# A graph layer pair on one core: one-hot tables made six tiles at a time, basis parts spread anew

## What is computed

```python
# layer 0
xw = x @ W.T
out = segment_sum(dinv[row] * dinv[col] * xw[row], col) + b
x = _layernorm(x + gelu(batch_norm(out)) + x)

# layers 1 and 2: rgcn_gate_layer
w = einsum('rb,bio->rio', att, basis)      # 30 matrices of 512 x 512, 2 relations
for r in range(2):
    gate = sigmoid(x_j @ gate_w[r, :, 0])
    msgs.append(gate[:, None] * x_j @ w[r])
msg = where(edge_type == 0, msgs[0], msgs[1])
out = segment_sum(msg, row) + x @ root + bias
```

## Time and profile before

| | us |
|---|---|
| median of 3 runs (327.39, 329.15, 327.48) | 327.48 |
| the profiled execution, whole | 326.88 |
| its span, first to last instruction | 325.0 |
| PE busy / DVE busy / ACT busy | 283.5 / 175.3 / 135.3 |
| mean granted TensorE clock | 0.942 of full |
| moved by DMA | 73.68 MB |

### The profile page before, as it was taken

How to read it: one execution, slowest core, us unless ns; L and a number is a source line. 1 busy time by engine, 2 the same in 40 slices (tenths; PEclk the granted TensorE clock), 3 DMA queues, 4 the chain that set the end, 5 groups by cost and what they waited for, 6 DMA issues and landing times.

```text
span 325.0 us, 4963 instructions
## 1 busy us (share of the span) xinstructions
PE 283.5 (87%) x1711; PEld 193.4 (60%) x1711; DVE 175.3 (54%) x538; ACT 135.3 (42%) x265; POOL 36.5 (11%) x71
## 2 busy tenths in 40 slices
PE   1768899885969999568999999999997999999991
PEld 1653455432336786424767656647795777787771
DVE  3878787999967847686310132233325125433333
ACT  4596868899701368647243114111313142100000
POOL 1001000000002900551000000000003600010000
PEclk9987999998695999779999999999998999999997
DMA  6974869599997999739998677975001400001112
GB/s 175 335 327 158 336 257 356 207 388 416 352 385 282 314 354 418 313 103 367 382 381 318 260 292 303 418 294 246 2 0 32 132 0 0 2 0 33 33 34 63
DMA packets 12759, 73.68 MB, mean 227 GB/s; under 512 B 1952, under 2 KB 2195, under 8 KB 4540
## 3 DMA queue, kind: packets, MB, share of 16 engines
q1 hardware_dynamic: 11282, 70.82, 57.4%
q0 software_dynamic: 1104, 2.36, 2.8%
q10 hardware_dynamic: 346, 0.17, 0.3%
HBM read 72.05 MB, written 1.28 MB: 226 GB/s over the span
## 4 chain that ended last, share of the span: by engine, by line
PE 61%; DVE 22%; issue 7%; DMA 4%; DVEq 2%; ACT 1%; POOL 1%; ACTq 0%; POOLq 0%
PE psW L495 13%; PE psM L476 10%; PE psM L477 9%; PE psM L478 9%; PE psM L717 6%; PE psM L737 6%; DVE oh_key L1047 4%; DMA basis_ring<-in_L_gnn_basis_dram 3%; PE psM L623 3%; DVE B L1038 2%; PE psE L570 2%; DVEq L1032 2%; DVE w L1027 1%; DVE x_sum L1170 1%; DVE AT L1103 1%
## 5 line engine op out<-in xcount | busy, mean ns | idle before, releaser
L495 PE MATMUL psW<-basis_ring,S 128*32 128x512 f32 x512 | 68.2, 651 | 3.2 <-DMA basis_ring<-in_L_gnn_basis_dram 3.1
L1217 DVE SCALAR_TENSOR_TENSOR zg<-psM,gate,zg 125x512 fp32r<-125x512 f32 x20 | 15.0, 751 | 59.5 <-ACT zg L891 59.5
L1047 DVE TENSOR_SCALAR oh_key<-iota_f,key 128x160 f16<-128x160 f16 x162 | 36.0, 262 | 2.6 <-PE psE L570 1.4
L785 ACT ACTIVATE oh_diff<-iota_f,edgeT 128x128 f16<-128x128 f16 x108 | 34.1, 389 | 3.4 <-DVEq L964 3.4
L495 PEld LDWEIGHTS psW<-basis_ring,S 128*32 128x32 f32 x512 | 13.9, 115 | 32.5 <-issue 26.4
L476 PE MATMUL psM<-w,hlT 128*125 128x512 f32 x80 | 33.1, 414 | 0.1
L891 ACT ACTIVATE zg<-psM,gate 125x512 fp32r<-125x512 f32 x20 | 13.8, 688 | 46.1 <-PE psM L478 45.7
L477 PE MATMUL psM<-w,hlT 128*125 128x512 f32 x80 | 32.3, 404 | 0.0
L478 PE MATMUL psM<-w,hlT 128*125 128x512 f32 x80 | 32.1, 402 | 0.0
L570 PEld LDWEIGHTS psE<-oh_key,oh_src 128*125 128x125 f16 x162 | 16.0, 150 | 25.2 <-issue 19.2
L570 PE MATMUL psE<-oh_key,oh_src 128*125 128x160 f16 x162 | 21.3, 261 | 10.2 <-issue 6.6
(11 more groups left out here) (159 smaller groups left out, 430.5 us busy)
## 6 DMA issues: line engine op xcount, KB each, us to landing
basis_ring<-in_L_gnn_basis_dram SPq DMA_DIRECT2D x64, 1024.0 KB, 7.1
root_raw<-in_L_gnn_root_dram POOLq DMA_DIRECT2D x32, 64.0 KB, 3.6
xs<-in_x_dram SPq DMA_DIRECT2D x1, 1120.0 KB
out_dram<-xs SPq DMA_DIRECT2D x5, 224.0 KB
w_raw<-in_L_gnn_W_dram SPq DMA_DIRECT2D x1, 1024.0 KB, 10.9
bias_b<-in_L_gnn_bias_dram POOLq DMA_DIRECT2D x1, 250.0 KB, 3.8
xs<-in_x_dram SPq DMA_DIRECT2D x1, 130.0 KB
out_dram<-xs SPq DMA_DIRECT2D x5, 26.0 KB
```

Source lines behind the costliest of these rows:

```text
L495: m = nc.tensor.matmul(psW[32 * j:32 * j + 32, cc % 2, :], S[:, cc % 2, cc // CH, q].rearrange("p k r -> p (k r)"), ring[:, n % RING, j, : ...
L785: nc.scalar.activation(oh_diff[:, g % 3, j * P:(j + 1) * P], iota_f[:, 0:P], ACT.Abs, bias=edgeT[:, 0, g * G + j:g * G + j + 1], scale=-1. ...
L1047: v.tensor_scalar(oh_key[:, t % OH, :], iota_f[:, 0:KEYS], key[:, t:t + 1], None, ALU.is_equal) \
```

## The change

The VectorE compares of a group become two instructions. `key_pairs` and `place_pairs` hold each edge's key and place twice side by side in 16 bits (two casts over 324 elements ahead of the loop). A `tensor_tensor` compare then reads the counting row in pairs, repeated over the tiles, and each tile's pair, repeated over the row: 6 x 160 = 960 elements for the keys, 4 x 126 = 504 for the places. ScalarE keeps two places (GA = 2, `Relu` over 256 columns). `oh_key` grows from 12 to 18 tiles (three groups). TensorE waits for a whole group's keys, VectorE for the whole group three before. The register reads of a group's two windows stand ahead of its compares, and the two window adds follow each other behind them.

The product `xw` is spread over 20 groups, one part each. Basis parts in the edge loop drop from 24 to 16, two every three groups from group 5; then 2 after the degrees, 2 after dinv, 8 in the aggregation, 2 behind the transposes `g`, 6 while the layer norm's result is turned, 8 in root1, 14 in Z, 6 in layer 1's aggregation. The block steps move along: the edge loop holds block 0 and `w_first(1)` only; `w_merge(1)` stands behind `z`, `w_first(2)` ahead of the BB copies, `w_high(1)` and `w_low(1)` in f = 1, `w_merge(2)` in f = 2, `w_high(2)` and `w_first(3)` ahead of the last GELU, `w_low(2)` and `w_merge(3)` behind the third `x1_lo`. `w_merge` gains a wait for `w_lo` of the block before.

```diff
-OH = 12
-GA = 4
+OH = 3 * G
+GA = 2
+PLACES = PC + PC % 2
...
+        PARTS_IN = 15
-        FIRST_AT = {8: 0, 17: 1}
-        HIGH_AT = {13: 0, 22: 1}
-        MERGE_AT = {11: 0, 20: 1}
-        LOW_AT = {14: 0, 23: 1}
+        MERGE_AT = {16: 0}
+        LOW_AT = {19: 0}
...
                 pe.wait_ge(src_ready, g + 1)
+                pe.wait_ge(key_ready, g + 1)
...
-                    pe.wait_ge(key_ready, t + 1)
...
-                if FIRST_XW <= g < FIRST_XW + NC * KC // 2:
-                    xw_part(2 * (g - FIRST_XW))
-                    xw_part(2 * (g - FIRST_XW) + 1)
-                basis_upto(9 * g // 10)
+                if FIRST_XW <= g < FIRST_XW + NC * KC:
+                    xw_part(g - FIRST_XW)
+                basis_upto(min(2 * g // 3 - 2, PARTS_IN))
...
-            basis_upto(24)
...
-            basis_upto(25)
+            basis_upto(17)
...
-            basis_upto(26)
+            basis_upto(19)
...
-                basis_upto((28, 30, 31, 32)[f])
-            basis_upto(33)
+                basis_upto((21, 23, 25, 27)[f])
...
+            basis_upto(29)
...
-                basis_upto((35, 36, 37)[c])
+                basis_upto((31, 33, 35)[c])
...
-                    basis_upto(39 + KC * h + f)
+                    basis_upto((37, 37, 39, 39, 41, 41, 43, 43)[KC * h + f])
...
-                    basis_upto(min(60 + KC * h + f, 2 * CH * SUB - 1))
+                    basis_upto((57, 59, 59, 61, 61, 63, 63, 63)[KC * h + f])
...
             act.wait_ge(z_ready, NC)
+            w_first(2)
...
-                if f == 2:
+                if f == 1:
+                    w_high(1)
+                if f == KC:
                     w_high(2)
                     w_first(3)
...
+            v.tensor_copy(place_pairs[:], edgeT[:, 0, :].unsqueeze(2).broadcast_to([P, T, 2]))
...
+            link(v.tensor_copy(key_pairs[:], key[:].unsqueeze(2).broadcast_to([P, T, 2])))
...
+            def one_hots(out, pairs, first, n, width):
+
+                pair = iota_f[:, 0:width].rearrange("p (k i) -> p k i", i=2)
+                shape = [P, n, width // 2, 2]
+                return v.tensor_tensor(out, pair.unsqueeze(1).broadcast_to(shape),
+                                       pairs[:, first:first + n].unsqueeze(2).broadcast_to(shape), ALU.is_equal)
+
+            for g in range(NG):
+                if g >= 3:
+                    dve.wait_ge(adj_used, G * (g - 2))
+                at = [window_at(w) for w in range(2 * (g - 2), 2 * (g - 1))] if g >= 2 else []
+                src = oh_src[:, g % 3].rearrange("p (t e) -> p t e", t=G)[:, GA:, 0:PLACES]
+                one_hots(src.rearrange("p t (k i) -> p t k i", i=2), place_pairs, g * G + GA, G - GA, PLACES)
+                one_hots(oh_key[:, g * G % OH:g * G % OH + G].rearrange("p t (k i) -> p t k i", i=2), key_pairs, g * G, G, KEYS) \
                     .then_inc(key_ready, 1)
...
-            w_merge(2)
             wait_full(dve, "deg")
...
+            w_merge(1)
             for h, (c0, c1) in enumerate(((0, 4), (4, NC))):
...
-                if c == 1:
-                    w_merge(3)
...
-            w_low(3)
+            w_low(2)
+            w_merge(3)
```

More of the change, by code:

```diff
@@ L805, in _ @@
                 places(g)
[L806 to L813 removed]
                 for i in TURNED_LOW_AT.get(g, ()):
                     turned_high(i)
[L816 removed]
+                if g in range(FIRST_XW + 5, NG, KC):
+                    xw_out((g - FIRST_XW - 5) // KC)
+                if g in (10, 22):
+                    w_first(g // 12)
+                if g == 18:
+                    w_high(0)
             wait_full(act, "vec")
@@ L1052, in _ @@
                     dve.wait_ge(b_zero, 1)
-                if t % G == G - 1:
-                    for i in TURNED_LOW_AT.get(t // G, ()):
-                        turned_low(i)
-                if t == ROUNDS_AT * G:
-                    rounds()
-                if t % G in (1, 3) and t > 2 * G:
-                    add_window(t // SG - 4)
-                if t % G == 3 and t // G in MERGE_AT:
-                    w_merge(MERGE_AT[t // G])
-                if t % G == 3 and t // G in LOW_AT:
-                    w_low(LOW_AT[t // G])
+                for i in TURNED_LOW_AT.get(g, ()):
+                    turned_low(i)
+                for i, w in enumerate(range(2 * (g - 2), 2 * (g - 1)) if g >= 2 else ()):
+                    add_window(w, at[i])
+                if g == ROUNDS_AT:
+                    rounds()
+                if g in MERGE_AT:
+                    w_merge(MERGE_AT[g])
+                if g in LOW_AT:
+                    w_low(LOW_AT[g])
             for w in range(NW - 4, NW):
-                add_window(w)
+                add_window(w, window_at(w))
             dve.wait_ge(win_added, NW)
@@ L1143, in _ @@
                         bn_finish(f - 1)
-                if f == 2:
-                    w_low(2)
                 link(last)
@@ L1153, in _ @@
                 link(v.tensor_tensor(bn[:, 3, e], vecT[:, 1, f, V_B:V_B + 1], bn[:, 3, e], ALU.subtract))
+                if f == 1:
+                    w_low(1)
+                if f == 2:
+                    w_merge(2)
             bn_finish(KC - 1)
@@ L1207, in _ @@
             v.tensor_tensor(gw_hl[:, :, :, 1], gw, gw_hl[:, :, :, 0].bitcast(F32), ALU.subtract).then_inc(gw_ready, 1)
+            w_low(3)
             w_merge(4)
```

38 lines of the change are left out of this document (14 added, 24 removed).

## The result

The changed kernel takes **349.17 us** (median of four runs, 349.02 to 349.58) against 327.44 for the kernel before beside it (326.6 to 329.15): a ratio of 1.066, 95% interval 1.062 to 1.070. The forecast was 317, with a range to 326, so even the sign was wrong. The profiled execution has a span of 346.9 us, with a mean clock of 0.952 (0.942 before).

The account below looks back on a forecast made before the run. It took three engines in the edge loop as near their limits, TensorE leading until 65 us, then VectorE. Loop -13.9, (a) to (e) 0.0, (f) +2.0, (g) +1.9 gave -10.0 us: 317, likeliest 313 to 321, eight in ten 307 to 326.

Parts of the forecast that it names:

- The register reads: Edge loop: with reads ahead of the compares, VectorE's idle time ahead of its adds goes, -5.2 us (0 to -5.2).
- Compares: Edge loop, VectorE: two new compares take 0.83 us a group instead of 1.34, -13.8 us over 27 groups.
- one element a cycle: Rival, edge loop: pairs engage no faster mode, compares go from -13.8 to +8.4 us, whole 337 us; chance 0.12.
- The adds together: Edge loop, VectorE: the second add waits 0.30 us for the first, 0.85 us a pair, +9.8 us over 25 pairs.
- Edge loop: Whole edge loop: VectorE's sum of -12.4 us and another -1.5 from fewer waits for TensorE, -13.9 us.
- (a): Behind the edge loop, at the degrees: `w_merge(2)` leaves, so their copy comes earlier, -0.9 us.
- (e): Layer norm, where VectorE leads: `w_merge(3)` leaves it, -2.4 us.
- (g): Layer 1's aggregation: it gains a pair of basis parts with TensorE full, +1.9 us.
- (b): Behind the edge loop: basis parts 18 and 19 stand ahead of the aggregation, +1.86 us.
- (d): Ahead of the last GELU: `w_high(2)` and `w_first(3)` take 1.97 + 1.28 us against 1.81 of ScalarE idle, +1.4 us.
- (f): From the transposes `g` to root1: the ring of basis transfers decides, not TensorE, +2.0 us (0 to +6).
- the ring gives the gain back: Rival, behind the loop: 48 parts left instead of 40, +4 and +2 us, whole 323; chance 0.15, shared with longer waits.

Follow-up runs that it names:

- e1: The changed kernel with a group's two register reads moved behind its two compares; 332.39 us.
- e3: The kernel before with only the new compares, reads ahead of them and adds together; product, basis parts and block steps at their old places; 339.10 us.
- e5: The kernel before with the new compares and adds together, old schedule, but the two register reads behind the compares; 325.07 us.
- e11b: The changed kernel with VectorE's group in the order key compare, read, add, place compare, read, add; 326.73 us.
- e6: e1 with the transfers of basis parts 16 to 63 at half their bytes, so the result isn't the reference's; 324.4 us.
- e9b: e5 with the transfers of basis parts 16 to 63 at half their bytes, so the result isn't the reference's; 324.9 us.
- e7: e1 with ScalarE's `w_high(2)` and `w_first(3)` behind the last GELU of layer 0 instead of ahead of it; 334.36 us.
- e8: e5 with VectorE's group reordered to key compare, read, add, place compare, read, add; old schedule; 319.36 us.

## Why the prediction was wrong, point by point

**The register reads, -5.2 forecast: the step that failed.** The text says that with the reads ahead of the compares VectorE's idle time "goes". It looked at what the reads had cost behind the compares (5.2 us in 54 adds) and not at what stands in front of them at the new place. Before, a read was issued while three key compares ran, 0.52 us, about as long as it takes itself, so nearly all of it was hidden. At its new place only an add is left ahead of it. The cost was +0.68 us a group against e1 (2.65 - 1.97), 17.6 us of loop (14.1 with the old schedule, e3 against e5). In place of 5.2 us of idle time less, VectorE had 26.2 ahead of the place compares. The order of instructions that stands ahead of the prediction shows the two `TENSOR_LOAD`s at the head of the group; the prediction gave them no price there.

**Compares, 0.83 us a group forecast: right.** The steps are 0.34 + 0.57 = 0.91. By the records, (652 - 421) / (960 - 504) = 0.51 ns an element, a third above the lower bound's 0.375 and half the upper's 1.04. (The prediction's lower-bound total, -15.0, comes to -15.3 by its own numbers; nothing hangs on it.) The rival "one element a cycle" didn't come true. The Trainium skill's rule in "VectorE: DVE Perf Modes", The perf-mode tier table, two elements a cycle for this form, gave an estimate of 0.50 us for 960 elements, 0.52 ns each. The trace agrees with 0.51.

**The adds together, 0.85 us a pair forecast: a little too dear.** From the first add of a pair to the next compare it is 56.12 - 55.43 = 0.69 in e1. Parting them together with the reads (e1 to e11b) brought 6.5 us, 0.26 a group; how much of that is the wait between the adds and how much the 0.30 of reads was not taken apart.

**Edge loop, -13.9 forecast, +10.9 measured.** The changed kernel's 106.1 less the 17.6 of the reads' place is 88.5, less the 6.5 of the parting 82.0. The forecast was 81.3, and that e11b comes so close is in part luck, since its order of the group is another one. The forecast summed 0.83 + 0.85 = 1.68 us a group; e1's group is 1.97, the difference being the 0.30 of reads that two compares don't cover (the errors of compares and adds cancel). That TensorE would allow it held: with VectorE out of the way (e11b) it let the loop end at 82.

**Behind the loop, +3.9 forecast, +11.0 measured** (12.5 against e3). The terms (a) to (e) and (g) came to 1.9, and without the ring it is 5.2 (e6 against e9b in the table of stages). Up to the transposes it is 2.0, where (a), (b) and (d) had 2.4. In the changed kernel the aggregation starts 13.0 us behind `AT` and 12.0 before, (a) being -1.0 (the degrees' copy 6.63 us behind `AT` instead of 7.64) and (b) +1.9. From the transposes to root1 it is -0.6 where (e) had -2.4; two parts more stand in the same stretch, and why the rest didn't come wasn't tested. In root1 it is +1.6, for which the sum had no term: e6's TensorE waits 1.44 us there for the `w_merge` that the change puts behind `w_low(2)`. From layer 1's aggregation to the end it is +2.1 where (g) had 1.9; in the changed kernel this part takes 107.1 us and in e5 105.2, +1.9. The steps ahead of the GELU have no better place behind it, since there they delay `xs` (e7).

**(f), the ring: +2.0 forecast with +6 as its end, 9.5 measured in e1 and 6.9 in the changed kernel.** This term was mis-sized. The working counted the ring only from the layer norm on ("Here the ring decides, not TensorE"). But 8 parts more are left behind the loop, eight times 2.49 us, and the waits begin in the aggregation (at 125.5 and 134.6 us), where the forecast put only TensorE's 1.86 for a pair. The rival "the ring gives the gain back" named this mechanism, with 4 us on top of 2.

**What would show it.** The line "if the compares are fast but `AT` late, the adds or TensorE's clock" had the symptom and neither cause: the adds were cheaper than forecast, and the clock was 0.89 in both stretches of the loop shown, as in the last one of the earlier trace rows. "It is the ring if `AT` comes early and the end doesn't" describes e11b exactly. ScalarE did idle ahead of `oh_src`, and Z started later than before, at 194 us, not 12 us earlier.

## What to carry to other kernels

A register read is an instruction with a price and a place: look in the engine's order at what is queued ahead of it, and keep at least its own length of work there, in particular where the instruction ahead waits for something. When instructions are merged into fewer and longer ones, the gaps between them, in which reads and chained waits were hidden, go too; e8 got most of its gain from putting the long ones back in between. Before work that needs transfers is moved out of one stage into later ones, count the bytes that go with it against the later stages' transfer time from the first of them on, not only where the engine already waits for transfers.
